# Counting edges with one-hot products: column one-hots for two and three groups by one comparison, and PSUM moved in twos and threes

## The reference, cut to what matters

```python
edge_index = jnp.stack([src, dst])          # 103125 edges, sorted by dst
z = jax.ops.segment_sum(alpha[:, None] * h[src], dst, num_segments=N)
...
mask = jnp.concatenate([edge_type == r, jnp.ones((N,), dtype=bool)])
```

## Time and profile before

| What | us |
|---|---|
| Median of three runs | 2724.74 |
| The profiled execution, its own time | 2725.16 |
| Its span | 2723.3 |
| Count stage, first to last L326 start (124 fives) | 393.0 |
| The same, per five | 3.17 |
| VectorE busy, 84 to 456 (372 long) | 367.67 |
| TensorE granted clock, 84 to 456 (share of 2.4 GHz) | 1.00 |

### The profile page before, as it was taken

The page is one execution under the profiler, slowest core; times in us unless marked ns, Lnnn a source line. Parts: engine busy times, 40 slices in busy tenths (PEclk is TensorE's granted clock), DMA queues, the critical chain, the costliest instruction groups (busy, mean ns, idle before and its releaser), DMA issues. The chain is left out here.

```text
span 2723.3 us, 90169 instructions
## 1 busy us (share of the span) xinstructions
PE 2103.4 (77%) x33923; PEld 1853.3 (68%) x33923; DVE 2161.7 (79%) x4355; ACT 1860.7 (68%) x3006; POOL 86.7 (3%) x137
## 2 busy tenths in 40 slices
PE   3999997698698698395938999489976989567544
PEld 3655554598598597394927999389875889566522
DVE  6999996788788788515078999899988999759943
ACT  5999997675775775202059999699969999445431
POOL 1111111000000000000000000000000000000000
PEclk8999998899899899697978999799988999788767
DMA  3354554342342341272722331333304332043100
GB/s 85 158 225 196 206 224 196 120 142 65 114 150 62 119 148 59 86 220 66 236 80 83 113 100 35 101 106 95 95 21 129 96 95 83 4 140 121 41 9 24
DMA packets 182241, 302.56 MB, mean 111 GB/s; under 512 B 6394, under 2 KB 158845, under 8 KB 181976
## 3 DMA queue, kind: packets, MB, share of 16 engines
q1 hardware_dynamic: 181191, 297.57, 33.0%
q0 software_dynamic: 800, 1.26, 0.2%
HBM read 214.26 MB, written 84.54 MB: 110 GB/s over the span
## 5 line engine op out<-in xcount | busy, mean ns | idle before, releaser
L430 ACT ACTIVATE stage<-ps 125x375 f32 x625 | 313.9, 603 | 38.1 <-PE ps L376 33.8
L331 DVE TENSOR_SCALAR col<-iota_col,window_col 125x376 bf16<-125x376 f16 x1250 | 310.0, 318 | 3.6 <-PE ps L376 3.6
L376 PE MATMUL ps<-col,lo 125*125 125x375 bf16 x1250 | 290.3, 345 | 17.5 <-DVE col L331 17.2
L931 ACT ACTIVATE r1amsk<-r1ad,r1thr 125x640 f16 x360 | 259.6, 816 | 0.1
L931 ACT ACTIVATE r2amsk<-r2ad,r2thr 125x640 f16 x360 | 259.6, 814 | 0.1
L931 ACT ACTIVATE r0amsk<-r0ad,r0thr 125x640 f16 x360 | 259.6, 814 | 0.1
L1004 PE MATMUL ps<-r1mv,r1asel 125*128 125x66 f16 x5000 | 244.4, 196 | 4.8 <-issue 3.5
L1004 PE MATMUL ps<-r2mv,r2asel 125*128 125x66 f16 x5000 | 242.7, 196 | 2.4 <-issue 1.3
L1004 PE MATMUL ps<-r0mv,r0asel 125*128 125x66 f16 x5000 | 242.8, 196 | 1.1 <-DVE r0asel L953 0.5
L376 PEld LDWEIGHTS ps<-col,lo 125*125 125x125 bf16 x1250 | 136.9, 139 | 144.5 <-DVE col L331 141.4
L1004 PEld LDWEIGHTS ps<-r1mv,r1asel 125*128 125x128 f16 x5000 | 227.4, 100 | 8.7 <-issue 4.0
(11 more groups left out here) (537 smaller groups left out, 4412.5 us busy)
## 6 DMA issues: line engine op xcount, KB each, us to landing
counts<-stage SPq DMA_DIRECT2D x75, 800.0 KB, 4.8
ct<-counts_all SPq DMA_DIRECT2D x75, 800.0 KB, 4.6
counts_all<-total SPq DMA_DIRECT2D x25, 800.0 KB, 7.3
g0ct<-counts_all SPq DMA_DIRECT2D x25, 800.0 KB, 4.7
g1ct<-counts_all SPq DMA_DIRECT2D x25, 800.0 KB, 4.6
g2ct<-counts_all SPq DMA_DIRECT2D x25, 800.0 KB, 4.6
r0ct<-counts SPq DMA_DIRECT2D x25, 800.0 KB, 4.7
r1ct<-counts SPq DMA_DIRECT2D x25, 800.0 KB, 5.3
```

The costliest lines, as they stand in the source:

```text
L331: ins = v.tensor_scalar(col1[:, b % OHS * WIN + w], K.iota_col[:], K.window_col[:, bass.ds(i * (P // DG) + b, 1), w], None, ALU.is_equal)
L376: ins = pe.matmul(K.ps[0:P, s, 0:GW], lo1[:, b, 0:P, w], col1[:, s * WIN + w, 0:GW], start=(w == 0), stop=(w == WIN - 1))
L430: act.activation(dst.rearrange("p a r h d -> p (a r h) d"), K.ps[0:P, b % OHS, 0:GW].rearrange("p (x d) -> p x d", d=DG), ACT.Copy).then_i ...
L931: act.activation(msk[:, s % 5, n], ad[:, bass.ds(g % 2, 1), h] .rearrange("p a (b d) -> p (a b) d", d=PAD), ACT.Sigmoid, bias=T.thr[:, 1, ...
```

## The change

The column one-hot is made interleaved (w innermost), by the same kind of two-input comparison as `lo1`: against a ramp `iota_pair` that is now 376 long, one instruction for the first two groups of a five (1504 elements a partition) and one for the other three (2256). It is written to `col2`, a view of `col1` with three slots of a five each, and `hot` goes up by two and by three. VectorE waits on `counted` once a five, with thresholds 5, 10, 10, 15, 20 and a start of 10. TensorE reads the moving operand at L376 from `col2`, every second element, and all 128 columns of `lo1` and of the identity as stationary operand. ScalarE moves banks 0 and 1 by one copy (750 elements) once both are counted, and banks 2, 3 and 4 by another (1125), and raises `taken` by two and by three; `move_total` follows at the same place. `window_col` becomes f16. The waits of TensorE and the place of `add_up` stay as they are.

```diff
--- before.py
+++ after.py
@@ -98,7 +98,7 @@
         si = sb("si", [P, NG], I32)
         order = sb("order", [P, NG], F16)
         ki = sb("ki", [P, GE], I32)
-        pi = sb("pi", [P, PAD, 2], I32)
+        pi = sb("pi", [P, GE, 2], I32)
         wt = sb("wt", [D, 6, D], F32)
         a = sb("a", [D, 6, 8], F32)
         m = sb("relm", [128, 2], F32)
@@ -142,7 +142,7 @@
                 pool.iota(gi[:], [[P, DG]], channel_multiplier=1).then_inc(iotas, 1)
                 pool.iota(ti[:], [[GW, NG]], channel_multiplier=0).then_inc(iotas, 1)
                 pool.iota(ki[:], [[1, GE]], channel_multiplier=0).then_inc(iotas, 1)
-                pool.iota(pi[:], [[1, PAD], [0, 2]], channel_multiplier=0).then_inc(iotas, 1)
+                pool.iota(pi[:], [[1, GE], [0, 2]], channel_multiplier=0).then_inc(iotas, 1)
                 pool.wait_ge(rows_ready, 1)
                 pool.wait_ge(keys_out, 32)
@@ -295,7 +295,8 @@
     with ExitStack() as ctx:
         sb = lambda name, shape, dt: ctx.enter_context(nc.sbuf_tensor(name, shape, dt))
         lo1 = sb("lo1", [P, P // DG, PAD, WIN], BF16)
-        col1 = sb("col1", [P, SLOTS, GE], BF16)
+        col1 = sb("col1", [P, 30, GE], BF16)
+        col2 = col1[:].rearrange("p s c -> p (s c)").rearrange("p (a s c w) -> p a s c w", a=3, s=OHS, w=WIN)
         stage, total = K.stage, K.total
         lo_wide = lo1[:].rearrange("p s l w -> p (s l w)")[:, 0:SLOTS * PAD].rearrange("p (s l) -> p s l", l=PAD)
         (hot, counted, taken, summed, stored, diag, wide_hot, wide_used, moved) = (
@@ -318,20 +319,19 @@
                 wide = v.value_load(K.wide[0:1, 0:1], min_val=0, max_val=1)
                 with v.If(wide < 1):
                     with v.Fori(0, NB) as i:
-                        for b in range(P // DG):
-                            v.wait_ge(counted, i * (P // DG) + b + 1)
-                            if b % OHS == 0:
+                        for n in range(P // DG // OHS):
+                            v.wait_ge(counted, i * (P // DG) + (5, 10, 10, 15, 20)[n])
+                            groups = bass.ds(i * (P // DG) + OHS * n, OHS)
+                            v.tensor_tensor(
+                                lo1[:, OHS * n:OHS * n + OHS], K.iota_pair[:, 0:PAD].unsqueeze(1).to_broadcast([P, OHS, PAD, WIN]),
+                                K.window_lo[:, groups].unsqueeze(2).to_broadcast([P, OHS, PAD, WIN]), ALU.is_equal)
+                            for s0, s1 in ((0, 2), (2, OHS)):
+                                own = bass.ds(i * (P // DG) + OHS * n + s0, s1 - s0)
                                 v.tensor_tensor(
-                                    lo1[:, b:b + OHS], K.iota_pair[:].unsqueeze(1).to_broadcast([P, OHS, PAD, WIN]),
-                                    K.window_lo[:, bass.ds(i * (P // DG) + b, OHS)].unsqueeze(2)
-                                    .to_broadcast([P, OHS, PAD, WIN]), ALU.is_equal)
-                            for w in range(WIN):
-                                ins = v.tensor_scalar(
-                                    col1[:, b % OHS * WIN + w], K.iota_col[:],
-                                    K.window_col[:, bass.ds(i * (P // DG) + b, 1), w], None, ALU.is_equal)
-                            ins.then_inc(hot, 1)
+                                    col2[:, n % 3, s0:s1], K.iota_pair[:].unsqueeze(1).to_broadcast([P, s1 - s0, GE, WIN]),
+                                    K.window_col[:, own].unsqueeze(2).to_broadcast([P, s1 - s0, GE, WIN]),
+                                    ALU.is_equal).then_inc(hot, s1 - s0)
                 with v.Else():
                     with v.Fori(0, NG // OHS) as i:
                         for s in range(OHS):
@@ -349,7 +349,7 @@
             @block.tensor
             def _(pe):
-                pe.sem_inc(counted, OHS)
+                pe.sem_inc(counted, 2 * OHS)
                 pe.sem_inc(moved, 1)
                 def add_up(i, n, own=True):
@@ -359,8 +359,8 @@
                     pe.wait_ge(moved, 5 * i + n + 1)
                     for half, (h0, h1) in enumerate(HALVES):
                         for r in range(R):
-                            ins = pe.matmul(K.ps[0:P, OHS + half, 0:(h1 - h0) * NB], K.ident16[0:P, 0:P],
-                                            stage[0:P, bass.ds(slot, 1), r, h0:h1, bass.ds(25 * q, 25)]
+                            ins = pe.matmul(K.ps[:, OHS + half, 0:(h1 - h0) * NB], K.ident16[:],
+                                            stage[:, bass.ds(slot, 1), r, h0:h1, bass.ds(25 * q, 25)]
                                             .rearrange("p a h d -> p (a h) d"), start=(r == 0), stop=(r == R - 1))
                     ins.then_inc(summed, 1)
@@ -373,7 +373,7 @@
                             pe.wait_ge(taken, i * (P // DG) + b + 1)
                             for w in range(WIN):
-                                ins = pe.matmul(K.ps[0:P, s, 0:GW], lo1[:, b, 0:P, w], col1[:, s * WIN + w, 0:GW],
+                                ins = pe.matmul(K.ps[:, s, 0:GW], lo1[:, b, :, w], col2[:, b // OHS % 3, s, 0:GW, w],
                                                 start=(w == 0), stop=(w == WIN - 1))
                             ins.then_inc(counted, 1)
                             if b in ADDED:
@@ -389,7 +389,7 @@
                             with pe.Fori(0, STEPS) as c:
                                 pe.wait_ge(wide_hot, i * (OHS * STEPS) + s * STEPS + c + 1)
                                 for w in range(SLOTS):
-                                    ins = pe.matmul(K.ps[0:P, s, 0:GW], lo_wide[:, w, 0:P], col1[:, w, 0:GW],
+                                    ins = pe.matmul(K.ps[:, s, 0:GW], lo_wide[:, w], col1[:, w, 0:GW],
                                                     start=False, stop=False, skip_group_check=True)
                                 ins.then_inc(wide_used, 1)
@@ -416,22 +416,22 @@
                         act.wait_ge(stored, 64 * i + 64 * (STAGES - 1))
                     slot, q = (i % 2, n - 1) if n else ((i + 1) % 2, 4)
                     for half, (h0, h1) in enumerate(HALVES):
-                        ins = act.activation(total[0:P, bass.ds(slot, 1), h0:h1, 25 * q:25 * q + 25]
+                        ins = act.activation(total[:, bass.ds(slot, 1), h0:h1, 25 * q:25 * q + 25]
                                              .rearrange("p a h d -> p (a h) d"),
-                                             K.ps[0:P, OHS + half, 0:(h1 - h0) * NB].rearrange("p (h d) -> p h d", d=NB),
+                                             K.ps[:, OHS + half, 0:(h1 - h0) * NB].rearrange("p (h d) -> p h d", d=NB),
                                              ACT.Copy)
                     ins.then_inc(moved, 1)
                 with act.Fori(0, NB) as i:
                     act.wait_ge(stored, 64 * i + 64)
-                    for b in range(P // DG):
-                        act.wait_ge(counted, i * (P // DG) + b + 1 + OHS)
-                        dst = stage[0:P, bass.ds(i % STAGES, 1), :, :, DG * b:DG * (b + 1)]
-                        act.activation(dst.rearrange("p a r h d -> p (a r h) d"),
-                                       K.ps[0:P, b % OHS, 0:GW].rearrange("p (x d) -> p x d", d=DG),
-                                       ACT.Copy).then_inc(taken, 1)
-                        if b - 1 in ADDED:
-                            move_total(i, ADDED.index(b - 1))
+                    for n in range(P // DG // OHS):
+                        for s0, s1 in ((0, 2), (2, OHS)):
+                            act.wait_ge(counted, i * (P // DG) + OHS * n + s1 + 2 * OHS)
+                            dst = stage[:, bass.ds(i % STAGES, 1), :, :, DG * (OHS * n + s0):DG * (OHS * n + s1)]
+                            act.activation(dst.rearrange("p a r h (s d) -> p s (a r h) d", d=DG),
+                                           K.ps[:, s0:s1, 0:GW].rearrange("p s (x d) -> p s x d", d=DG),
+                                           ACT.Copy).then_inc(taken, s1 - s0)
+                        move_total(i, n)
                 move_total(NB, 0)
             @block.sync
@@ -1442,9 +1442,9 @@
                 K.keys = sb2("keys", [P, NCH, 2], F32)
                 K.group_base = sb2("group_base", [P, NG], F32)
                 K.iota_col = sb2("iota_col", [P, GE], F16)
-                K.iota_pair = sb2("iota_pair", [P, PAD, WIN], F16)
+                K.iota_pair = sb2("iota_pair", [P, GE, WIN], F16)
                 K.window_lo = sb2("window_lo", [P, NG, WIN], F16)
-                K.window_col = sb2("window_col", [P, NG, WIN], F32)
+                K.window_col = sb2("window_col", [P, NG, WIN], F16)
                 K.wide = sb2("wide", [1, 1], I32)
                 K.stage = sb2("stage", [ROWS, STAGES, R, NB, PAD], F16)
                 K.total = sb2("total", [ROWS, 2, NB, PAD], F16)
```

## The result

The changed kernel takes 2802.42 us (median of four runs, 2801.98 to 2803.42) against 2725.1 for the kernel before: ratio 1.0257, 95% interval 1.0216 to 1.0298. It is 77 us slower. (The ratios in this document are estimates over all executions; they need not equal the ratio of two medians.) Forecast were 35 us, 2760, with a range of 2732 to 2807: the sign and the place were right and the time lies in the range, but the forecast change is less than half of the one that came. The profiled execution took 2801.98 us, its span is 2800.2.

A forecast was written before the change was run, and what follows sets the result against it. VectorE bounded the kernel before at 3.17 us a five; a ring of ScalarE's move of three and TensorE would replace it at 3.44. 124 x (3.44 - 3.17) = 33.5, plus 1.6, gave 35 on 2725.16: 2760 us, range 2732 to 2807.

The forecast's parts named there:

- the ring: Move of three, third group, fourth, `add_up`, fifth, move of three: one turn a five, 3.44 us (3.31 to 3.82); chance 77%.
- the move of 1125 elements: ScalarE's copy of banks 2, 3 and 4: taken at 1.25 us, low bound 1.12, high bound 1.55.
- VectorE after: L326 at 0.74 us plus two comparisons of 0.85 and 1.23: 2.82 us a five, against 3.17 before.
- TensorE's part: From the third group's first weight load through `add_up` and the fifth group to the next move's start: 2.14 us.
- the hop: From the end of a ScalarE instruction to TensorE's first weight load: 0.13 us.
- 128 columns: Faster TensorE weight loads: 0.08 us less a five, 0.05 in `add_up` and 0.03 at the first load.
- Small parts: Later first product, longer last move, longer ramps and f16 keys: about 1.6 us together, nothing to 3.
- The half-rate rival: At L376 TensorE reads every second moving element at half rate, steps 0.31 us for 0.16: 2877 us; chance 9%.
- the two rules that the prediction names beside this rival: Skill pages on L376's operand: any non-contiguous access slows matmuls, giving 2877; or the 16-bit limit is step 8, giving 2760.
- The clock: Rival: TensorE's pauses of about 0.6 us a turn drop the clock to 1.2 GHz: 2970 us; chance 2%.
- GpSimd's first instruction took long, so I add nothing for it: L326 beside GpSimd stepped 0.74 us as well, GpSimd's first instruction took 0.93; nothing was added to VectorE's 2.82.
- My faster rival: VectorE stays the bound, the ring turns in under 3.17 us, the saved comparisons show in full: 2684 us; chance 8%.

The follow-up runs named there:

- the moves alone: The kernel before with only ScalarE's moves changed, to twos and threes: 2793.72 us, ratio 1.0256.
- the two ways of opening it: Changed kernel, identity added by VectorE: with one move a group, 2695.74 us; with moves in twos and threes and `add_up` behind the fifth group, 2692.16 us.
- single_moves: The changed kernel with one ScalarE move a group again, GpSimd's additions kept: 2831.19 us, ratio 1.0392.
- before_loops_on_vector: The kernel before with the identity added by VectorE instead of GpSimd, nothing else changed: 2716.12 us, ratio 0.9934.

## Why the prediction was right or wrong

The step that failed is a term of the ring's sum, the move of 1125 elements: taken at 1.25 us, it lasts 1.45. The mechanism stood. Term by term:

- **VectorE after, 2.82 us a five**: right. Comparisons 0.935 and 1.327, and 2.83 where VectorE runs free.
- **The ring takes its place**: right, shown by the moves alone (2793.72) and by the two ways of opening it, each with GpSimd out of the stage (2695.74 and 2692.16). Where GpSimd stayed, both ways of opening it gave more than the changed kernel (2831.19 and 2819.34), by the starvation, which the prediction did not have.
- **TensorE's part, 2.14, and the hop, 0.13**: right, 2.15 and 0.11.
- **The move of 1125 elements, 1.25 us**: this is the term that failed; it measured 1.45 in the mean (1447 ns in the group row above), nearer to my high bound of 1.55. I took something between two durations of a one-group move and added pure elements. But the spread in the earlier trace rows, 490 to 751 ns, was two kinds of move: in the kernel before the 325 moves of groups that don't straddle last 0.49 to 0.59 us, the 300 that do 0.66 to 0.75, and none lies between. In the timeline of the kernel before, two neighbours:

```profile
205.66 0.53 ACT L430 ACTIVATE stage<-ps 125x375 f32 x1
206.03 0.70 ACT L430 ACTIVATE stage<-ps 125x375 f32 x1
```

  The slow kind's 0.17 is a cost of the group, not of the instruction, so a move of three has it once or twice: 8 of the 15 groups in a block's moves of three straddle, 1.6 a move. 1.18 without it (0.17 below the shorter, 1.35), and 1.6 x 0.17 = 0.27: 1.45. The 1.18 is 0.06 above my low bound of 1.12, and my 1.25 had 0.13 above it for all else; so the straddling is most of the miss. The missed 0.20 makes 0.20 x 124 = 25 us.
- **128 columns, -0.08 us**: right for the first load (0.03), wrong for `add_up` (0.05). It stepped 0.83 with loads of 0.133 us and of 0.096, so its loads did not set its step. 0.05 x 124 = 6 us.
- **Small parts, 1.6 us**: 8 measured (76.9 of span less 68.7 in the turns, by one block). 1.3 of them are there before the stage (L186 starts at 32.21 before, at 33.53 after). They come from the longer ramp, which the prediction put at 0.1 at most on GpSimd: GpSimd's IOTA takes 1.24 us longer, and a cast of VectorE that runs beside it, unchanged, ends 0.45 us behind it in both kernels, before

```profile
13.66 1.03 POOL L145 IOTA pi<- 125x256 int32 x1
14.18 0.96 DVE L170 CAST zT<-ei 125x825 f32<-125x825 int32 x1
```

  and after:

```profile
13.73 2.27 POOL L145 IOTA pi<- 125x752 int32 x1
14.25 2.20 DVE L170 CAST zT<-ei 125x825 f32<-125x825 int32 x1
```

  Another 1.3 lie between L186 and the first L419 (32.21 to 65.37 before, 33.53 to 67.98 after). From the last L419 of the loop to the first L460 it is 529.58 to 550.05 for 456.35 to 473.70, 3.1 longer, in waits that I had not costed; 5.5 us of that stretch go when GpSimd's last additions do. The later stages last 0.5 longer. The remaining 2 are in the turns after all: over all 124, from the first L419 of the loop to the last, the kernel before takes 390.98 us and the changed one 461.60, 70.6 more and not 68.7.
- **The half-rate rival**: not so. Four matmuls over every second element take 0.83 us in the timeline above, the last one alone 0.33, so they step (0.83 - 0.33) / 3 = 0.17, as before within the rows' rounding. Of the two rules that the prediction names beside this rival, the one that gives 2877 does not hold for this operand. **The clock** did not fall, though TensorE paused 1.1 us a turn. Stretch 84 to 500 of the changed kernel (columns as in the earlier trace rows):

```profile
84.00:500.00 416.00, 300.97 (x1788) 163.62 (x1786) 321.84 (x338) 325.15 (x447) 144.94 (x89) 1.00 0.42 173
```

- **"GpSimd's first instruction took long, so I add nothing for it"**: right for the block period of this kernel, and wrong as a reading. That row, 0.93 us, was the sign that VectorE's two-input instructions hold GpSimd up: it too ended 0.29 us after VectorE's L326 (209.16 + 0.82 = 209.98, and 209.34 + 0.93 = 210.27). In the changed kernel its first addition of a block lasts 5.57 us (218.06), and three blocks' room in `stage` hides it (the period of a block stays 18.61 without the additions). My faster rival, 2684 with VectorE as the bound, could not have come with GpSimd's additions where they are: with the ring open and VectorE full, GpSimd starves, and the kernel gave 2831.

The Trainium skill (SBUF — State Buffer, SBUF: two separate sides) says that VectorE with two SBUF inputs and a GpSimd operation that reads SBUF exclude each other for a whole instruction. The runs agree, and show more: in seven blocks of single_moves GpSimd did not get in between VectorE's instructions either, for 21.9 us, until VectorE paused (in eight others it did, after some 1.5 us). The comparisons of before, beside which GpSimd came in sooner, have one such input and are also shorter, 0.3 us; no run separates the two.

## What to carry to other kernels

When moves are merged, ask which later work waits for the merged move, and draw the ring: what stands in it (here a summation put between the fourth and fifth group) is paid every turn, though no engine is full. Before an engine is made to run without pauses, look for who lives on its pauses: one addition at 0.93 instead of 0.43 us in the trace of before was the only warning. And a duration with two values is two costs; find what chooses between them before it is scaled. When a kernel is changed in one stage, compare that stage by its own starts: here up to half of a difference of 10 us lay in a stage that nobody had touched.

## What the runs showed of the hardware

- GpSimd's addition of 125 x 125 elements, 0.42 us alone, lasted up to 21.9 us while VectorE ran two-input comparisons of 0.8 to 1.3 us back to back, and ended 0.28 us after VectorE's last one (single_moves). It was not always so long: other blocks' three additions took 3.55 us in the same run. Beside VectorE's one-input comparisons of 0.3 us, in the kernel before, the two took turns: GpSimd's four additions took 2.11 us and cost VectorE 0.68 us a block.
- ScalarE's writes in runs of 10 bytes cost 0.17 us more per 75 runs when each straddles a 16-byte boundary (0.85, 1.02 and 1.19 us for none, one and two groups of two).
- A reduction over partitions on GpSimd started 5.3 us after its input when GpSimd had run additions before it, and 0.1 us after it when it had not (before and before_loops_on_vector); what lies in these 5.3 us no run shows.
- TensorE read its moving operand in steps of two 16-bit elements as fast as adjacent ones: a step of 0.17 us for 375 columns against 0.16, at the clock's upper level (granted 1.00).
